# Graph layers on one core: one branch for all layers, a row of carried maxima, first rows kept in place

## What is computed

```
h = relu(layernorm(x)); x = x + L0(h, edge_attr_64)    # sum of relu(h[src] + attr @ We + be) by dst, MLP, batch norm
h = relu(layernorm(x)); x = x + L1(h)                  # mean of h[src] by dst, linear, relu
h = relu(layernorm(x)); x = x + L2(h, edge_attr_128)   # attention with 8 heads, LayerNorm, feed-forward, LayerNorm
h = relu(layernorm(x)); x = x + L3(h)                  # two attention layers: 4 heads of 32, then 1 head of 128

# attention, per head:
logits = ...[src] + ...[dst] (+ attr term)
m      = segment_max(logits, dst)
w      = exp(logits - m[dst])
out    = segment_sum(w * rows[src], dst) / segment_sum(w, dst)
```

## Time and profile before

| | us |
|---|---|
| Median of the runs | 5819.16 |
| Runs | 5816.36, 5819.16, 6398.47 |
| The profiled execution, its own time | 5822.44 |
| Its span, first to last instruction | 5818.2 |
| Setup | 0 to 69 |
| Layer 0, norm1 | 70 to 1143, 1144 to 1210 |
| Layer 1 | 1211 to 2300 |
| Layer 2, FFN | 2300 to 3413, 3414 to 3630 |
| Layers 3 and 4 | 3631 to 4724, 4725 to 5814 |

### The profile page before, as it was taken

How to read it: one execution, slowest core, us unless ns; L and a number is a source line. 1 busy time by engine, 2 the same in 40 slices (tenths; PEclk the granted TensorE clock), 3 DMA queues, 4 the chain that set the end, 5 groups by cost and what they waited for, 6 DMA issues and landing times. The chain is left out here.

```text
span 5818.2 us, 90194 instructions
## 1 busy us (share of the span) xinstructions
PE 4591.7 (79%) x21959; PEld 3150.7 (54%) x21959; DVE 2713.5 (47%) x8261; ACT 1217.7 (21%) x3182; POOL 3999.1 (69%) x4207
## 2 busy tenths in 40 slices
PE   4888888757777775999999976687777757778777
PEld 3777777545555554444444433455555545555555
DVE  4222222231111112777777766555555545555555
ACT  2111111131222111222222258111111111111111
POOL 5777777557777774777777710777777747777775
PEclk9999999999555555999999989666767656666665
DMA  4333333244444443555555511455545524444443
GB/s 143 105 105 104 104 105 104 75 146 105 116 109 113 114 105 86 168 167 165 166 166 166 165 39 25 112 112 114 113 112 116 115 71 106 111 110 110 109 111 78
DMA packets 559448, 663.86 MB, mean 114 GB/s; under 512 B 196415, under 2 KB 390381, under 8 KB 558317
## 3 DMA queue, kind: packets, MB, share of 16 engines
q1 hardware_dynamic: 424509, 382.99, 22.2%
q0 software_dynamic: 134640, 277.80, 20.9%
HBM read 580.95 MB, written 86.19 MB: 115 GB/s over the span
## 5 line engine op out<-in xcount | busy, mean ns | idle before, releaser
L1784 POOL DMA_INDIRECT soft_rows<-table,sources x2496 | 2393.3, 959 | 1126.0 <-issue 1114.1
L1414 POOL DMA_INDIRECT sum_rows<-table,sources x832 | 787.9, 947 | 346.1 <-issue 341.5
L1080 POOL DMA_INDIRECT term_rows<-table,sources x832 | 794.6, 955 | 300.3 <-issue 300.3
L1915 PE MATMUL psum<-soft_onehot,soft_message 128*128 128x64 f32 x3328 | 646.6, 358 | 134.3 <-DVE soft_message L2059 131.9
L1915 PEld LDWEIGHTS psum<-soft_onehot,soft_message 128*128 128x128 f32 x3328 | 585.3, 265 | 214.7 <-issue 208.9
L1111 PE MATMUL psum<-term_onehot,term_term 128*128 128x64 f32 x1664 | 403.8, 424 | 192.5 <-DVE sums L1163 183.7
L1456 PE MATMUL psum<-sum_onehot,sum_rows 128*128 128x64 f32 x1664 | 361.8, 392 | 222.3 <-DMA sum_rows<-table,sources 218.5
L1111 PEld LDWEIGHTS psum<-term_onehot,term_term 128*128 128x128 f32 x1664 | 370.5, 328 | 246.1 <-issue 245.9
L1157 DVE TENSOR_TENSOR term_term<-psum,term_rows 128x512 f32<-128x512 f32 x208 | 143.8, 691 | 756.8 <-issue 363.2
L1456 PEld LDWEIGHTS psum<-sum_onehot,sum_rows 128*128 128x128 f32 x1664 | 345.7, 305 | 276.6 <-issue 272.4
L1911 PEld LDWEIGHTS psum<-soft_onehot,soft_weights 128*4 128x4 f32 (+1 forms) x3328 | 283.9, 108 | 305.8 <-issue 292.3
(11 more groups left out here) (278 smaller groups left out, 6633.8 us busy)
## 6 DMA issues: line engine op xcount, KB each, us to landing
soft_onehotT<-onehotsT SPq DMA_DIRECT2D x312, 256.0 KB
soft_onehot<-onehots SPq DMA_DIRECT2D x624, 128.0 KB
soft_attrs<-in_ea128T SPq DMA_DIRECT2D x208, 256.0 KB
soft_rows<-table,sources POOLq DMA_INDIRECT x2496, 2.6
term_attrs<-in_ea64T SPq DMA_DIRECT2D x208, 128.0 KB
onehots<-term_onehot SPq DMA_DIRECT2D x208, 128.0 KB
sum_onehot<-onehots SPq DMA_DIRECT2D x208, 128.0 KB
onehotsT<-sum_flat SPq DMA_DIRECT2D x208, 128.0 KB
```

What stands on the lines that cost most here:

```text
L1080: pool.indirect_dma_start(rows[:, k, t, :], None, io.table0[0:NCH * CN], bass.IndirectOffsetOnAxis(sb.sources[:, g * TPG + t:g * TPG + t + ...
L1414: pool.indirect_dma_start(rows[:, k, t, :], None, io.table1[0:NCH * CN], bass.IndirectOffsetOnAxis(sb.sources[:, g * TPG + t:g * TPG + t + ...
L1784: pool.indirect_dma_start(rows[:, k, t, :], None, table[0:NCH * CN], bass.IndirectOffsetOnAxis(sb.sources[:, g * TPG + t:g * TPG + t + 1], ...
L1915: last = pe.matmul(bank[:, 0:W], message[:, g.slot(4), b, :], onehot[:, k, b], start=b == 0, stop=b == TPG - 1)
```

## The change

1. `edge_phase` is gone. `build` loads `narrow` once behind `first_phase` and branches once. The narrow side holds all layers one behind the other, the Else holds all layers in the general form. `norm1_phase` and `ffn_phase` stand in both, so they take a name.
2. `carry` is one row of G + 1 values a head. The scan of a batch writes its four places in it, from an offset that changes with the loop, and starts from the value before them. The copy is gone, and `s.carry` is counted once a batch in place of twice.
3. In the setup, `rows` is gone: `rows_out` writes into `sb.sums`, which holds nothing yet and is as large as all rows, and waits for no store. All stores count one semaphore, awaited at the end.
4. x comes in three loads: chunks 0 to 2, chunk 3, the rest. `statistics` of chunk 3 waits for the second; the wait for the rest stands behind `rows_out` of chunk 1, the last VectorE instruction of the step in which chunk 3's statistics are.

```diff
 first_phase
-        rows = tile("rows", [P, 2, TPG, D])
+        def kept_rows(c):
+            return sb.sums[:, nodes_of(c)].rearrange("p (b f) -> p b f", b=TPG)
...
-                sp.dma_start(sb.x[:, (STATIC - 1) * TPG:, :], x_blocks[:, (STATIC - 1) * TPG:, :]).then_inc(s.x_rest, 16)
+                sp.dma_start(sb.x[:, (STATIC - 1) * TPG:STATIC * TPG, :], x_blocks[:, (STATIC - 1) * TPG:STATIC * TPG, :]).then_inc(s.x_next, 16)
+                sp.dma_start(sb.x[:, STATIC * TPG:, :], x_blocks[:, STATIC * TPG:, :]).then_inc(s.x_rest, 16)
...
-                    sp.dma_start(table_rows(io.table0, c), rows[:, k]).then_inc(s.stored[k], 16)
+                    sp.dma_start(table_rows(io.table0, c), kept_rows(c)).then_inc(s.stored, 16)
...
-                sp.wait_ge(s.stored[0], 16 * (CH - CH // 2))
-                sp.wait_ge(s.stored[1], 16 * (CH // 2))
+                sp.wait_ge(s.stored, 16 * CH)
...
                     if c.i is None and c.base == STATIC - 1:
-                        v.wait_ge(s.x_rest, 16)
+                        v.wait_ge(s.x_next, 16)
                     norm.statistics(v, c, blocks_of(sb, c), s.h)
...
                     v.wait_ge(s.h[k], c.nth())
-                    freed(v, s.stored, c, 16)
-                    v.tensor_tensor(rows[:, k], h[:, k], sb.L0_be..., ALU.add).then_inc(s.rows[k], 1)
+                    v.tensor_tensor(kept_rows(c), h[:, k], sb.L0_be..., ALU.add).then_inc(s.rows[k], 1)
+                    if c.i is None and c.base == STATIC - 3:
+                        v.wait_ge(s.x_rest, 16)
 soft_sweep
-        carry = tile("carry", [H, 2, BATCH + 1])
+        carry = tile("carry", [H, G + 1])
...
                     if g.back(BATCH).exists():
-                        v.wait_ge(s.carry, g.back(BATCH).uses(BATCH, 2))
-                    v.tensor_tensor_scan(carry[:, q, 1:1 + BATCH], sb.inside[0:H, bass.ds(g.times(1), BATCH)], carry_bank, carry[:, q, 0:1],
-                                         ALU.add, ALU.max).then_inc(s.carry, 1)
-                    v.wait_ge(s.carry, g.uses(BATCH, 2) - 1)
-                    v.tensor_tensor(shift, carry[:, q, 0:BATCH]...
+                        v.wait_ge(s.carry, g.back(BATCH).uses(BATCH))
+                    v.tensor_tensor_scan(carry[:, bass.ds(g.times(1, 1), BATCH)], sb.inside[0:H, bass.ds(g.times(1), BATCH)], carry_bank,
+                                         carry[:, bass.ds(g.times(1), 1)], ALU.add, ALU.max).then_inc(s.carry, 1)
+                    v.wait_ge(s.carry, n)
+                    v.tensor_tensor(shift, carry[:, bass.ds(g.times(1), BATCH)]...
-                    v.tensor_copy(carry[:, 1 - q, 0:1], carry[:, q, BATCH:BATCH + 1]).then_inc(s.carry, 1)
 build
         first_phase(nc, io, sb)
-        edge_phase(nc, io, sb, 0)
-        norm1_phase(nc, io, sb)
-        edge_phase(nc, io, sb, 1)
-        edge_phase(nc, io, sb, 2)
-        ffn_phase(nc, io, sb)
-        edge_phase(nc, io, sb, 3)
-        edge_phase(nc, io, sb, 4)
+        narrow = nc.values_load(sb.narrow, min_val=0, max_val=1)
+        with nc.If(narrow > 0):
+            narrow_layers(nc, io, sb)
+        with nc.Else():
+            wide_layers(nc, io, sb)
```

More of the change, by code:

```diff
@@ L330, in first_phase @@
              "widest", "widest_T", "narrow", "att", "inside", "cont", "behind",
-             "norm_loaded", "x_first", "x_rest", ln=2, root=2, h=2, transposed=2, kept=2, rows=2, stored=2)
+             "norm_loaded", "x_first", "x_next", "x_rest", "stored", ln=2, root=2, h=2, transposed=2, kept=2, rows=2)
     x_blocks = io.x.rearrange("(b p) f -> p b f", p=P)
@@ L462, in rows_out @@
                     v.wait_ge(s.h[k], c.nth())
-                    freed(v, s.stored, c, 16)
-                    v.tensor_tensor(rows[:, k], h[:, k], sb.L0_be.unsqueeze(1).broadcast_to([P, TPG, D]), ALU.add).then_inc(s.rows[k], 1)
+                    v.tensor_tensor(kept_rows(c), h[:, k], sb.L0_be.unsqueeze(1).broadcast_to([P, TPG, D]), ALU.add).then_inc(s.rows[k], 1)
+                    if c.i is None and c.base == STATIC - 3:
+                        v.wait_ge(s.x_rest, 16)
                 skewed(nc, v, 3, [(1, 0.0, lambda c: norm.scale_shift(v, c)), (0, 0.4, statistics), (2, 2.4, rows_out)])
@@ L522, in first_phase @@
     phase_end(nc, s)
[L525 to L544, removed]
+def narrow_layers(nc, io, sb):
+    term_sweep(nc, io, sb)
+    norm1_phase(nc, io, sb)
+    sum_sweep(nc, io, sb)
+    soft_sweep(nc, io, sb, 2)
+    ffn_phase(nc, io, sb)
+    soft_sweep(nc, io, sb, 3)
+    soft_sweep(nc, io, sb, 4)
+def wide_layers(nc, io, sb):
+    edge_sweep(nc, io, sb, 0, False)
+    mlp0_phase(nc, io, sb)
+    norm1_phase(nc, io, sb, "wide_norm1")
+    edge_sweep(nc, io, sb, 1, False)
+    layer1_phase(nc, io, sb)
+    edge_sweep(nc, io, sb, 2, False)
+    ffn_phase(nc, io, sb, "wide_ffn")
+    edge_sweep(nc, io, sb, 3, False)
+    gat_out_phase(nc, io, sb, False)
+    edge_sweep(nc, io, sb, 4, False)
+    gat_out_phase(nc, io, sb, True)
 def edge_sweep(nc, io, sb, layer, narrow):
@@ L1973, in _ @@
                 v.memset(starts[:, GE:GE + 1], 0.0).then_inc(s.cleared, 1)
-                v.memset(carry[:, 0, 0:1], 0.0).then_inc(s.cleared, 1)
+                v.memset(carry[:, 0:1], 0.0).then_inc(s.cleared, 1)
                 if not full:
@@ L2175, in mlp0_phase, with norm1_phase @@
     phase_end(nc, s)
-def norm1_phase(nc, io, sb):
-    s = sems(nc, "norm1", "ones", bn=2, plus_h=2, back=2, x_new=2, ln=2, root=2, h=2, transposed=2, kept=2, stored=2)
+def norm1_phase(nc, io, sb, name="norm1"):
+    s = sems(nc, name, "ones", bn=2, plus_h=2, back=2, x_new=2, ln=2, root=2, h=2, transposed=2, kept=2, stored=2)
     with ExitStack() as ctx:
-        tile = node_phase(nc, "norm1", ctx)
+        tile = node_phase(nc, name, ctx)
         norm = LayerNorm(tile, "ln", s.ln, s.root)
@@ L2411, in layer1_phase, with ffn_phase @@
     phase_end(nc, s)
[L2414 to L2417 removed]
+def ffn_phase(nc, io, sb, name="ffn"):
+    s = sems(nc, name, staged=2, node_major=2, den=2, inverse=2, attn=2, plus_h=2, ln1=2, root1=2, norm1=2, gain1=2, hh=2,
              hhT_psum=2, hhT=2, up=2, gelu=2, down=2, down_T=2, down_nodes=2, res=2, ln2=2, root2=2, norm2=2, gain2=2, shift2=2, x_new=2, ln3=2,
```

8 lines of the change are left out of this document (3 added, 5 removed).

## The result

The changed kernel takes 5803.63 us (median of 16 runs), the kernel before 5815.11 us (16 runs). The ratio is 0.9981, 95% interval 0.9974 to 0.9987: 11 us less, between 7.6 and 15.1, where 26.6 were predicted. One of the 16 runs of the kernel before took 6398.47 us and does not count in the ratio. The time lies in the predicted range, but the gain I worked out lies outside the interval, so a term is missing or wrong. The two profiled executions differ by another amount again: span 5818.2 before, 5796.6 after, 21.6 us. Both riddles are open at this point.

A forecast was written before the change was run, and what follows sets the result against it. GpSimd's gathers were taken to bound every layer over the edges but layer 2, which TensorE bounds. Setup 11.6, branch 15.0 and carry 0 sum to 26.6 us, giving 5793 us against the median; range 5780 to 5808 us.

The forecast's parts named there:

- setup: Setup phase: VectorE's wait on the table0 store goes and chunk 3 starts sooner; gain 11.6 us, bounds 9.2 and 13.6.
- into norm1: Border from layer 0 to norm1: VectorE's first add no longer comes late behind ScalarE's first tile; 1.9 us gained.
- layer 1 to layer 2: Border before layer 2: the jump's delay of 3.8 us and the load's 0.4 us go; 4.2 us gained.
- last jump: End of the kernel: the jump over the wide code, 4.26 us on TensorE's queue, stays; no gain.
- carry: Carried maxima in layers 2, 3 and 4: dropped copy against more register work, taken as 0; bounds -7 and +8 us.
- The stores no longer gate the compute: Setup: stores need 17 us at 200 GB/s, with 24 us left until the phase's new end at 57; no cost taken.
- straight code pays nothing: Borders: fetching runs ahead in sequence, so a border without a jump waits 0.0 us for code, against 3.9 with one.
- the change on VectorE is about nothing: Layers 2 to 4: three new register steps, some 0.15 us, offset the removed 0.13 us copies on VectorE.
- layer 2 still 20.5 us a batch: Sign that the prediction is right: a batch of sixteen gathers in layer 2 keeps its time of 20.5 us.
- the borders keep most of their price: Rival at the phase borders: straight code must also be fetched; gain 11.6 + 5, time 5802 us, chance 0.08.
- more gathers caught behind L2068: Rival in layer 2: each further gather held per batch costs 28 us, up to 5877 us in all; chance 0.06.
- the first two rivals: Slow store drain ending setup later (5801 us, chance 0.08); borders still paying to fetch straight code (5802 us, chance 0.08).

The follow-up runs named there:

- before_carryrow: The kernel before with only the carry part of the change (one row, no copy): 5818.79 us, ratio 1.0001.
- pads_oldcarry: The changed kernel with the old two-half carry and copy, and 80 more VectorE instructions at the head of layer 1: 5789.2 us, ratio 0.9948 to the kernel before.
- before_pad64: The kernel before with 128 more waits (64 instructions) on VectorE at the head of layer 1: 5827.35 us, ratio 1.002.
- before_setup: The kernel before with only the setup part (rows in the space of the sums, x in three loads): 5803.72 us, ratio 0.9977.
- after_pad128: The changed kernel with 256 more waits (128 instructions) on VectorE at the head of layer 1: ratio 0.9943 to the kernel before, on the slow chip.
- after_pads: The changed kernel with 96 more VectorE instructions at the head of layer 1 and 40 at layer 4: 5783.68 us, ratio 0.9942 to the kernel before.

## Why the prediction was right and wrong

The terms, in us of gain:

```
term                        predicted   measured
setup                         11.6       10.9
into norm1                     1.9        1.4   (VectorE's first add 2.3 sooner)
norm1 to layer 1               0.4        0.5
layer 1 to layer 2             4.2        4.3
layer 2 to FFN                 3.9        3.9   (ScalarE 4.3 sooner)
FFN to layer 3                 0.4        0.5
layer 3 to layer 4             4.2        4.3
last jump                      0          0.7
carry                          0          0     (before_carryrow), 1 to 2 (pads_oldcarry)
sum                           26.6       26.5
loop of layer 2 refetched      -        -13.8   (918.7 against 904.9, first to last branch)
```

**What held.** Each term that the prediction listed. A border without a jump costs its barrier and a start, on every engine. "The stores no longer gate the compute" holds: setup ends at 59.0. The chosen 0 for the carry holds within what can be told.

**What failed.** The step of the branch part that says straight code pays nothing, and the carry part's "the change on VectorE is about nothing". At the borders the first is true; inside layer 2 it is not. They priced instructions and jumps forward, and took the place of all other code as free. Moving the wide code out shifted VectorE's loop of layer 2 from instruction 2769 to 1904 of its program, where it touches four blocks. Each turn then costs some 2.7 us of silence on VectorE. TensorE, which is 97% busy there, loses the part that it can't make up: from the first of VectorE's twelve loop branches to the last it is 904.6 to 905.6 us in the six profiles with fast branches and 918.4 to 919.3 us in the four with slow ones (all but those on the slow chip). The means differ by 13.8 us, 1.3 us a round, and TensorE's wait for the product grew by 22.7 - 9.0 = 13.7 us. The prediction's sign "layer 2 still 20.5 us a batch" fails with it: a quarter of a round is 20.9 us after and 20.6 before.

The other 3 us of the 16.9 are not the loop's. They come from the first profile of the kernel before, in which the stretch from layer 2's barrier to the first of these branches took 174.1 us. In before_pad64, before_carryrow and before_setup, with the same border, it took 177.8 to 178.5. TensorE's granted clock from 45 to 60 us behind the barrier was 1.00 in the first and 0.68 to 0.77 in the three others, so that execution had the better clock there.

None of my rivals had this mechanism. The nearest, "the borders keep most of their price", put a fetch at the wrong place. The rival of more gathers caught behind L2068 did not come: the mean gather of layer 2 is 979 ns after (814.5 us / 832) and 980 before.

The kernel before had such stalls too: its branches in layers 3 and 4 took 2.7 to 3.6 us, eight times each. They stood in its trace, and cost nothing that can be told, because the gathers set the pace there: without the stalls, in before_pad64, these layers take 1088.6 and 1087.7 us, with them in before_setup 1089.7 and 1086.2. One turn in layer 3, timeline of VectorE in the kernel before:

```profile
4030.70 0.67 DVE L2059 TENSOR_TENSOR soft_message<-soft_rows,psum 128x512 f32<-128x512 f32 x1
4035.78 0.21 DVE L2001 TENSOR_SCALAR sums<-sums,soft_factor_of  x1 [4.42 <-issue]
```

The bracket says 4.42 us of issue, with the branch at 4030.8 in between. This row, read as a price of the loop's place, would have named the risk for layer 2.

The Trainium skill's page "Runtime: NRT & Kernel Launch" (Instruction fetch mechanics), which the prediction used for jumps, says that a taken branch whose target isn't in the current window of two pages must wait for a fetch. A loop's branch is a taken branch, so the rule covers it, and I had applied it to the far jumps alone. The same page of the Trainium skill gives blocks of 16 KiB, 256 instructions. The measurement differs. A loop of 342 instructions touches three blocks of 256 only if it begins in the last 85 places of one, so two starts 128 apart can't both be slow; after_pad128 shows them slow both times. Packets of 8.2 KB and blocks of 128 fit all 30 loops. Why four blocks are one too many is not shown; one more block fetched ahead of the branch would do it, and that it is the timing of that fetch which spared 4 of 11 turns on the slow chip is a guess.

**The two differences.** Between the two first profiles layer 2 counts with its 16.9 us, so the terms of the table make 26.5 - 16.9 = 9.6 of the 21.6 us. The other 12.0 lie in layers 0, 1, 3 and 4 (3.4 + 2.8 + 4.1 + 1.7, borders taken off). The gathers of these layers are busy 9.2 us less in sum: 794.6 to 791.4, 787.9 to 785.7, 788.4 to 786.3 and 789.5 to 787.8 (window view of both). Their median is 947 ns in the first profile of the kernel before and in after_pad128, and 944 or 945 ns in the twelve others, five of which are the kernel before, moved or not, or with one part of the change. So most of the 12 us belong to that one execution. Why an execution has 3 ns more in each gather stays open, and 2.8 us of the 12.0 have no row. The sum went out from this execution, 5822.44 us, and corrected 3.3 us for it; the median of 16 runs says 7.3. From 5815.1 the terms as predicted give 5788.5, with the 13.8 us of the loop it is 5802.3, and 5803.63 was measured; the gain is 26.5 - 13.8 = 12.7 us by the terms and 11.5 (7.6 to 15.1) by the times. That 5793 came out as near as it did owes something to two errors of opposite sign, the base and the missing loop. That the time lies in the range is in part luck: the bounds of the terms (a gain of 18 to 36 us) end at 5801, the first two rivals at 5802, and no row of the prediction stood for the stretch from there to 5808 in which the measured time lies.

With the stalls gone the gain is 5815.95 - 5783.68 = 32.3 us (26 to 42 by the interval): the 26.6 us of the terms are all there. The 5.7 us above them lie inside the interval; the last jump and the carry account for about 2 of them, and the rest stays open.

## What to carry to other kernels

Code that is moved, added or removed ahead of a long loop can change the loop's own time, though nothing in it changes. So test each part of a change alone, and look at the idle time between a loop's branch and its first instruction, on the engine with the longest loop body; where it is microseconds, move the loop by a few dozen instructions or shorten its body. A stall on an engine with slack is seen only if the bounding engine has none left: the same 2.7 us cost 1.3 us a round in layer 2 and nothing that could be told in layers 3 and 4. And before a difference between two profiles is called a cost, look whether a third profile of the same code repeats it: 3 us of the 16.9 did not.

## What the runs showed of the hardware that was not expected

- Behind the branch of a VectorE loop of 307 to 350 instructions the next instruction comes after 0.2 to 0.3 us if the loop touches three blocks of 128 instructions, and after 2.2 to 3.6 us (means) if it touches four; 30 loops of ten kernels, no exception.
- The same program had 11 of 11 slow turns in two executions and 7 of 11 in one on the slow chip.
- In layer 2 of the changed kernel three instruction packets start around each slow branch, the last 3.9 to 4.5 us behind it; with the loop moved (after_pads) none starts within 6 us of a taken branch.
- One chip took 7511 us for what the others do in 5816 with the same median gather of 944 ns; its DMA moved 89 GB/s over the span in place of 114.
- The median gather is 944, 945 or 947 ns by the execution. Over the four layers that gathers bound, 3 ns are 10 us, nearly the 11.5 us that this change gives.
